# A one-core attention and expert layer: row loads in another order, extra TensorE products at the start, and the first chunk's tail moved behind the maxima

## What is computed

```python
q = (x @ Wq.T + bq).reshape(B, T, 16, 8)            # k and v likewise
scores = einsum('bqhd,bkhd->bhqk', q, k) * scale    # masked within blocks of 64 tokens
out = einsum('bhqk,bkhd->bqhd', softmax(scores), v).reshape(B, T, C) @ Wo.T + bo
x = layernorm(x + out)
scores = sigmoid(x @ gate_w.T)                      # 4 of 8 groups, then 6 of 32 experts
combine = weights of the 6 experts, normalised, times 2.5
y = sum over e of combine[:, e] * (silu(x @ G_e.T) * (x @ U_e.T)) @ D_e.T + shared(x)
x = layernorm(x + y)
```

## Time and profile before

| | |
|---|---|
| median of 3 runs | 496.4 us (492.8 to 497.02) |
| profiled execution | 494.91 us, span of the instructions 493.1 us |
| mean granted clock | 0.901 |
| PE, DVE, ACT, POOL busy | 444.3 (90%), 350.3 (71%), 223.1 (45%), 141.9 (29%) us |
| chain that ended last | PE 73%, DVE 13%, DMA 4%, issue 3% |
| first unit, first E, last joined maxima, third `up` | 34.11, 71.57, 272.85, 319.09 us |

### The profile page before, as it was taken

How to read it: one execution, slowest core, us unless ns; L and a number is a source line. 1 busy time by engine, 2 the same in 40 slices (tenths; PEclk the granted TensorE clock), 3 DMA queues, 4 the chain that set the end, 5 groups by cost and what they waited for, 6 DMA issues and landing times.

```text
span 493.1 us, 7763 instructions
## 1 busy us (share of the span) xinstructions
PE 444.3 (90%) x2665; PEld 210.1 (43%) x2665; DVE 350.3 (71%) x848; ACT 223.1 (45%) x300; POOL 141.9 (29%) x244
## 2 busy tenths in 40 slices
PE   5429999999999999999799879899999999999992
PEld 2302232323333232433223323367676676666660
DVE  2619988888988888777987331286768869965863
ACT  4520016766857767677215369723242243223220
POOL 4061333756746362533213442400000000000000
PEclk9955558999999999998858869999999999999997
DMA  3434214420010101000000030033323322543330
GB/s 117 163 137 148 89 42 141 128 72 26 27 52 24 45 20 50 3 1 1 7 2 2 1 87 1 1 97 103 107 72 100 111 90 86 148 133 105 109 106 21
DMA packets 27031, 34.22 MB, mean 69 GB/s; under 512 B 5745, under 2 KB 16113, under 8 KB 26993
## 3 DMA queue, kind: packets, MB, share of 16 engines
q1 hardware_dynamic: 25862, 33.00, 21.7%
q10 hardware_dynamic: 1130, 0.74, 0.5%
HBM read 29.07 MB, written 4.46 MB: 68 GB/s over the span
## 4 chain that ended last, share of the span: by engine, by line
PE 73%; DVE 13%; DMA 4%; issue 3%; ACTq 3%; ACT 2%; POOL 2%; DVEq 0%; SPq 0%; POOLq 0%
PE ps L1338 13%; PE ps L1255 13%; PE ps L1380 11%; DVE mx L983 9%; PE ps L1353 6%; PE ps L1355 6%; PE ps L1354 6%; PE ps L1321 6%; PE ps L1251 6%; DMA rows_k<-scratch 2%; ACT probs L880 2%; ACTq L568 2%; PE ps L1268 1%; DMA wq<-in_wqT 1%; ACTq L603 1%
## 5 line engine op out<-in xcount | busy, mean ns | idle before, releaser
L983 DVE TENSOR_REDUCE mx<-ps 128x2 f32<-128x256 f32 (+3 forms) x384 | 191.0, 552 | 43.8 <-PE ps L1255 42.4
L880 ACT ACTIVATE probs<-ps 128x1024 f32<-128x1024 f32 (+2 forms) x160 | 142.8, 939 | 76.8 <-PE ps L1321 69.9
L1255 PE MATMUL ps<-rows_k,rows_q 48*128 48x128 bf16 (+3 forms) x576 | 117.6, 313 | 5.2 <-DVE mx L983 3.2
L1338 PE MATMUL ps<-probs,Vg 128*32 128x512 f32 (+3 forms) x768 | 86.8, 526 | 1.2 <-POOL probs L754 1.0
L923 ACT ACTIVATE rows_q<-ps 128x512 f32<-128x512 f32 x68 | 40.7, 599 | 97.3 <-PE ps L1355 94.7
L1255 PEld LDWEIGHTS ps<-rows_k,rows_q 48*128 48x128 bf16 x576 | 35.5, 97 | 91.6 <-DVE mx L983 65.9
L750 POOL TENSOR_SCALAR_AFFINE_SELECT probs<-probs 64x512 f32<-64x512 f32 x64 | 42.4, 662 | 110.4 <-ACT probs L880 108.9
L1353 PE MATMUL ps<-x1hi,w_hi 128*128 128x512 f32 x136 | 74.0, 544 | 0.0
L1321 PE MATMUL ps<-rows_q,rows_k 51*128 51x512 bf16 (+3 forms) x384 | 67.8, 347 | 4.0 <-ACT probs L880 3.9
L1380 PE MATMUL ps<-rows_k,w_down 128*128 128x512 f32 x136 | 69.5, 593 | 0.7 <-DVE rows_k L1199 0.7
L1194 DVE TENSOR_TENSOR rows_q<-ps,rows_q 128x512 f32<-128x512 f32 x64 | 44.1, 689 | 36.2 <-PE ps L1380 34.9
(11 more groups left out here) (105 smaller groups left out, 326.6 us busy)
## 6 DMA issues: line engine op xcount, KB each, us to landing
comb_rows<-weights SPq DMA_DIRECT2D x128, 128.0 KB, 3.0
scratch<-oT SPq DMA_DIRECT2D x8, 384.0 KB, 5.6
w_raw<-in_unitT SPq DMA_DIRECT2D x17, 128.0 KB, 5.7
rows_q<-scratch SPq DMA_DIRECT2D x16, 96.0 KB
rows_k<-scratch SPq DMA_DIRECT2D x14, 96.0 KB
w_down<-in_unitT SPq DMA_DIRECT2D x1, 1088.0 KB, 6.3
xT<-in_xT SPq DMA_DIRECT2D x4, 256.0 KB, 5.6
rows_q<-scratch SPq DMA_DIRECT2D x16, 64.0 KB
```

The lines of the kernel that those rows point to most:

```text
L880: act.activation(dst, src, ACT.Exp).then_inc(exps_ready, 1)
L983: dve.tensor_reduce(to, src, AX.X, ALU.max).then_inc(max_read, 1)
L1255: mm = pe.matmul(dst[:, at * m:(at + 1) * m], rows_q[f:f + ROWS, s, p + qt * P:p + (qt + 1) * P], rows_k[f:f + ROWS, s, p + k0:p + k0 + m] ...
L1338: mm = pe.matmul(ps[STRIP * j:STRIP * (j + 1), VALUES * BANK:VALUES * BANK + m], Vg[:, g % 2, kt, j, :], probs[:, (NB * g + b) % SLOTS, j, ...
```

## The change

Four edits:

1. In `load_q` and `load_k` the depth becomes the outermost loop of every source: 8 depths, then the parts (or copies), and the rows of q and k are permuted alike.
2. `keep_clock`: once the first value projection has been read from bank 4 and the identity has arrived, TensorE makes 22 products of the bf16 identity with 512 columns into bank 4, which nothing reads, and one more ahead of each unit among the first 66 banked steps (65 units and one top). The product stands behind the unit's wait for its bank.
3. The planner doesn't start a unit whose group is more than 1.6 groups ahead of the exponentials.
4. `TAIL_FROM` moves from unit 6 of group 6 to behind the last unit.

```diff
+WARM, WARM_UNITS = 22, 66
-TAIL_FROM = (NG - 2, 6)
+TAIL_FROM = (NG, 0)
@@ attention_order
+    lead = 1.6
@@ ready_m
+        if kind == "unit" and g + n / NM - i["e"] / NE > lead and i["e"] < len(ev):
+            return far
@@ load_q
-            part = scr[0, b, :, r, :].rearrange("h (d f p) t -> f h d (p t)", d=D, f=2)
+            part = scr[0, b, :, r, :].rearrange("h (d f p) t -> f d h (p t)", d=D, f=2)
             for f in range(2):
-                for at, n, src in ((0, 24, part[f]), (24, 16, part[f, 0:2]), (40, 8, part[f, 0])):
+                for at, n, src in ((0, 24, part[f]), (24, 16, part[f, :, 0:2]), (40, 8, part[f, :, 0])):
@@ load_k
-            part = scr[1, b, :, r, :].rearrange("h (d f p) t -> f h d (p t)", d=D, f=2)
+            part = scr[1, b, :, r, :].rearrange("h (d f p) t -> f d h (p t)", d=D, f=2)
-                for at, n, src in ((0, 24, part[f, 0:1].to_broadcast([3, D, PAIRS * T])),
-                                   (24, 16, part[f, 1:2].to_broadcast([2, D, PAIRS * T])), (40, 8, part[f, 2])):
+                for at, n, src in ((0, 24, part[f, :, 0:1].to_broadcast([D, 3, PAIRS * T])),
+                                   (24, 16, part[f, :, 1:2].to_broadcast([D, 2, PAIRS * T])), (40, 8, part[f, :, 2])):
@@ TensorE, behind the projections
+            def keep_clock(n):
+                for _ in range(n):
+                    pe.matmul(bank(VALUES), identb[:, :], parts[:, 0, 0, :], start=True, stop=True)
+
+            pe.wait_ge(masks_loaded, 32)
+            pe.wait_ge(v_ready, 1)
+            keep_clock(WARM)
@@ max_step
-                if r == 0:
-                    pe.wait_ge(masks_loaded, 32)
+                if r < WARM_UNITS:
+                    keep_clock(1)
```

## The result

The changed kernel is slower: 517.3 us (515.99 to 524.7, four runs) against 496.6, a ratio of 1.0425, 95% interval 1.0358 to 1.0492. The prediction was 483.3, in 475 to 492. One of the four, 524.7, is in a slower state that some executions of any kernel here fall into: a ratio leaves such runs out, a median and a range don't. The profiled execution took 517.64 us, its span is 515.9; before it was 493.1.

The account below looks back on a forecast made before the run. TensorE bounds the mixed stretch; at the low clock units are bounded nearly as much by reductions, and the first waits on loads. Start -2.7, units -17.9, behind them +9.0 make -11.6: 494.9 to 483.3 us, range 475 to 492.

Parts of the forecast that it names:

- A fall in the idle 23.6 to 26.5 that lasts a few us costs only 1 to 2: TensorE's idle time ahead of the first unit: a clock fall there would cost only 1 to 2 us.
- The 22 cost nothing: Products ahead of the units: they end at about 23.6 us, before the first unit, at no cost.
- I take it as held: Products beside the first units: the mix was assumed to keep the full clock, though no row showed such a mix.
- Rival (c): First units: clock not held, the 65 take about 67 us, 33 more; +17 in all, 511 us; chance 0.07.
- Edit 1: Row loads: the first unit starts at 26.5 us instead of 34.1, a gain of 7.6 us.
- Edit 2 at full clock: Products beside units: 0.64 us per masked unit, 6.7 us cost in all, first E at 70.4 us.
- The 1.5 us behind 70 us: Mixed work behind 70 us: a full clock there saves 1.5 us, bounds 0 and 2.5.
- the sum: Whole kernel: -2.7 at the start, -17.9 in the units, +9.0 behind them, together -11.6 us.
- Edit 3: Planner's limit on units running ahead: TensorE's order stays as it is, cost 0.
- Edit 4, units: Last two groups without the tail: 55.6 us like ordinary groups, last join at 255.0 instead of 272.85, -17.9 us.
- Behind the units: Chunk 1's tail up to the third `up`: it starts at 328.1 instead of 319.09, +9.0 us, bounds +4.9 and +16.
- The expert loop is the same: Work from the third `up` to the end: no change in time.

Follow-up runs that it names:

- e_alone: The changed kernel with 42 products ahead of the units instead of 22 and none beside them: 484.3 us, ratio 0.9782.
- e_warm42: The changed kernel with 42 instead of 22 products ahead of the units, the 66 beside units kept: 491.5 us, ratio 0.9898.
- e_late: The changed kernel with 20 more products behind the wait for the first rows, ahead of the first unit: 495.6 us, ratio 0.9991.
- e_half: The changed kernel with 42 products ahead of the units and the 66 beside units cut from 128 to 48 rows: 498.0 us in one run.
- e_loads_tail: The changed kernel without any product, keeping the new row loads and the tail behind the last unit: 481.5 us, ratio 0.9723.
- e_warm32: The changed kernel with 32 instead of 22 products ahead of the units, the 66 beside units kept: 487.9 us, ratio 0.9832.
- e_loads: The kernel before with only its row loads written depth outermost, no products, old place of the tail: 488.1 us, ratio 0.9855.

## Why the prediction was wrong

**The step that failed** is in the prediction's own words "A fall in the idle 23.6 to 26.5 that lasts a few us costs only 1 to 2", and with it "The 22 cost nothing: ... so they end at about 23.6, ahead of the first unit". The idle time was seen, but as 2.9 us, and it was 4.19: the 22 products ended at 23.0 and the first rows came at 27.2. No run tells whether 2.9 us would have kept the clock (1.71 did). Wrong above all was that the clock would come back by itself among the units: it stayed at 0.50 from 26.8 to 108.8 us, and in place of 1 to 2 us the first exponentials came 27.0 later than before (99.33 against 72.31) and the join of group 1 28.1. Of the mix of one product and one unit the prediction says "I take it as held", and it is held, but only from full clock; I asked of the mix one question, whether it holds the clock, and not the second, whether it can raise it. The row nearest to the second stood in the text: between 50 and 60 us of the kernel before TensorE is busy 9.61 of 10 us and stays at 0.50. I read it as "Units alone lose it", and it doesn't show that. In the kernel before the clock had fallen ahead of the first unit (34.11), while TensorE waited:

```profile
22.00:24.00 2.00, 0.00 (x0) 0.00 (x0) 0.00 (x0) 0.06 (x1) 0.00 (x0) 0.81 0.27 90
24.00:26.00 2.00, 0.00 (x0) 0.00 (x0) 0.00 (x0) 2.00 (x4) 0.00 (x0) 0.50 0.27 94
```

So the row shows units that don't raise a clock that is low already, and a low clock is what the changed kernel met behind its wait. That units alone also lose it only `e_alone` showed.

The Trainium skill (TensorE: Matmul & The Clock Gate, "HAM oscillation — how this bites in real kernels", in Part 1) tells of a kernel that loses the clock in each wait for a transfer. Here the trace agrees for the wait of 4.19 us. The same page of the Trainium skill ("What's actually happening", also there) has the clock follow how busy TensorE was; in the changed kernel it was busy 9.5 of 10 us for 80 us at 0.50, so the trace doesn't agree if busy means a product in flight.

**Rival (c)** is what happened, with a price of +17 and 511 us; it was given 0.07. Its parts: 65 units at the lower level in 67 us (measured from the product at 27.21 to the mask of the first unit without one at 94.38: 67.2), 33 more than before. What it lacked is 2.7 at the start (28.1 at the join of group 1, where its 33 less 7.6 make 25.4) and 3.2 at the end: +12.2 from the last join on instead of 9.0.

**Edit 1** was right: 26.5 forecast, 26.92 without products and 27.21 with them. Its worth alone, 7.2 us at the first exponentials, is all of the 7.2 that the first unit moved; it needs no other edit.

**Edit 2 at full clock** was right in its costs: 0.64 for a masked unit (27.71, 28.35 in `e_warm42`), first E at 71.27 against 70.4. The rule of the Trainium skill that was weighed there (TensorE: Matmul & The Clock Gate, "The mechanism" of Part 3), by which a masked unit would have paid 0.1 more, isn't borne out by the 0.64. The 1.5 us behind 70 us didn't come: the clock falls there again, to 0.66 (0.61 before), once the products beside units have ended. So even with the clock held, edit 2 takes back what edit 1 gave: the first exponentials come at 72.11, before at 72.31, and without products at 65.34. A span of 485.1 in `e_warm42` is 8.0 less than before where the sum said 11.6; 2.3 of the difference are the start (join of group 1 at 87.77, -0.4 instead of -2.7), 0.9 the end, 0.4 the units. The forecast of 483.3 would have been low by some 5 to 8 us against the medians with a held clock, too (487.9 and 491.5), and the same kernel without any product is faster than both (481.5).

**Edit 3** was set at 0 from the planner's order; it was not run alone and needs no run: the planner writes the same order with the limit and without it, for the changed kernel and for the old place of the tail.

**Edit 4, units**: -17.9 forecast, -17.5 measured; from the join of group 5 to the last 55.9 us, as the 55.6 of two ordinary groups. **Behind the units**: +9.0 forecast, +9.8 to the third `up`, which waits for the exponential of chunk 1's logits, as was said (the row at 339.51). The further 2.4 were put at nothing, as "The expert loop is the same". The two table loads in the chain are silu's first and the exponential's (337.68); silu's second, at 341.12, stands in no term. It comes when the third `up` has begun and stops the first experts, and 1.6 us go with it: that is the least that any kernel here with this third load needs more behind the third `up` than those without it. The rest goes with the clock, of which the sum had nothing either. In the changed kernel, `e_late` and `e_half` it is low for 3.4 us ahead of the third `up` (317.0 to 320.4 in the stretch below), where it stays at 1.00 in `e_loads_tail`, `e_alone`, `e_warm32` and `e_warm42`. It falls in all seven at the third `up`: in those four as that begins, in the three 1.4 to 1.7 us later, among the first experts. The stretch of the changed kernel:

```profile
310.00:325.00 15.00, 13.31 (x102) 5.33 (x102) 8.19 (x46) 10.51 (x13) 3.23 (x7) 0.89 0.19 42
```

Those four lose 8.1 to 8.3 up to the third `up` and 9.7 to 10.1 in all, the changed kernel, `e_late` and `e_half` 9.7 to 9.8 and 12.2. So the 9.8 beside the forecast 9.0 hold some 1.6 that go with the clock, and without them the forecast would have been 0.8 too high.

## What to carry to other kernels

Ask of any filler for the clock two things: does it hold the level, and does it raise it? A mix that holds may not raise, so a single wait of a few us ahead of it can decide all of the stretch behind it (here 65 units, 67 us); fill the wait to its end, or put a run of dense products behind it. And price the filler at full clock against the work at half clock: here units at half clock were bounded nearly as much by the reductions, and a filler that held the clock still cost: with the tail in the same place the ratios are 0.9832 and 0.9898 with it, 0.9723 without. The best kernels have none at all (476 us).

## What the runs showed that was not expected

The granted clock has a memory in this kernel: from 35 to 70 us two kernels run the same products and units at 0.50 and at 1.00, by what TensorE did before. A wait of 1.71 us left the clock at 1.00; one of 4.19 and one of 4.89 left 0.50. That isn't the two sides of one fixed limit. In `e_loads_tail`, whose wait lasted 8.47 us, the clock was down 2.1 us behind TensorE's last product (at 18.7), as the stretch below shows; in `e_loads` it took 5.0 us.

```profile
20.00:22.00 2.00, 0.00 (x0) 0.00 (x0) 0.62 (x1) 0.00 (x0) 0.00 (x0) 0.70 0.41 127
```

Twenty-one full-array products in a row brought it back within 7.2 us, while 65 of them, each with a unit of 48 rows behind it, didn't in 67 us. Products of 48 rows in the same number and length, with TensorE busy 10.00 of 10 us, lost it.
